# Retention in a six-block decoder: 16-bit parts for queries, keys and state, centring on ScalarE, row factors on GpSimd

## The chip, the cores and the metric

The kernel runs on one core of one Trainium2 chip. The metric is the device time of the whole program in microseconds (us). Three runs of the kernel before gave 1024.1, 1029.05 and 1029.89 us, median 1029.05 us.

## The reference

The program is a two-layer decoder over x of 2 sequences x 1024 tokens x 256 features. Each layer adds an attention, a cross attention and a feed-forward block to x, each on the layer-normalised x. The change touches only the attention of the second layer, a retention:

```
q, k (scaled), v, g = x @ q_w + q_b, ...      # 16 heads; q, k 16 wide, v 32 wide
qr, kr = theta_shift(q), theta_shift(k)       # x*cos + rotate_every_two(x)*sin
qk = einsum(qr, kr) * mask                    # mask: causal decay per head, rows scaled by 1/sqrt(row sum)
denom = clip(|sum of the row of qk|, 1, None)
out = einsum(qk / denom, v)
out = (out - mean) / sqrt(var + 1e-5)         # over each head's 32 values
return (silu(g) * out) @ o_w + o_b
```

## The kernel before

The function `retention` (line 2608) works through 16 tiles of 128 tokens, eight per sequence. Within a tile it makes the causal scores of all 16 heads; what lies further back comes through a running state `us` of key-value products, kept per head and decayed once a tile (recurrent form across tiles, attention form inside one). The decay mask is folded into the cosine and sine tables, so only an upper-triangle clearing is left for GpSimd.

All engines are programmed by hand, each with its own loop `for s in STEPS` from -2 to 18, and meet through semaphores (`wait_ge` and `then_inc`). **Each engine runs its own list in order**: an instruction that waits holds up everything behind it in that list. A step `s` works on several tiles at once (a software pipeline): the projections of tile s+2, the turned queries and keys of s+1, the scores of s, the outputs of s-1, the gate of s-2, the output projection of s-3.

- TensorE (lines 3026 to 3043): `score(s,0)`, `weigh(s-1)`, `qk(s+2)`, `score(s,1)`, `turn_qk(s+1,0)`, `output(s-3)`, `turn_qk(s+1,1)`, `values(s+1)`, `delta(s)`, `turn_z(s-2)`, `turn_x(s+4)`, `gates(s-1)`. `score` (L2922) multiplies 32-bit `qkT` by head; half 0 and half 1 of the heads share one PSUM tile `pss`, so half 1 waits for `lo_done`, the end of VectorE's `low(s,0)`. `weigh` (L2941) applies the scores, and L2937 applies the state copy `u` in 32 bits. `delta` (L3022) makes the new key-value products. `turn_qk` (L2996) transposes 32-bit `rot`.
- ScalarE (lines 2885 to 2902): `high(s,0)` (L2852, the high 16-bit part of the scores), `squares(s-1)` (L2843, L2845), `high(s,1)`, two `copy_turned` (L2859), `values(s+1)` (L2867 a 16-bit and L2868 a 32-bit copy), `z_high`, `x_high`, `silu(s-1)` (L2879).
- VectorE (lines 2812 to 2833): `low(s,0)` (L2726, the low part of the scores), `x_center(s+5)` (L2492), `gate(s-2)` (L2749, L2752), `rotate(s+2)` (L2779 to L2785), `low(s,1)`, `centre(s-1)` (four operations, L2762 to L2767, that make variance plus floor), `state(s)` (L2795, L2798), `add`, `z_low`, `values_low(s+1)` (L2734), `x_low`.
- GpSimd (lines 2707 to 2713): `mask(s,0)` and `mask(s,1)` (L2686, two instructions each), `power(s-1)` (L2705: (variance + floor) to the power -1/2, 16 numbers a partition), `expand(s)` (L2695: the state spread into the block layout `u`).

`high(s,j)` waits for the scores, `low(s,j)` for `high(s,j)`, `mask(s,j)` for `low(s,j)`, `weigh(s)` for both masks, and the second product of `gate` for `power`. DMA plays a part only at the start of the stage, for the tables.

Of the kernel before, what the change touches and what calls it, by code (L numbers as in the profile page):

```python
# [11 lines left out]
F16 = mybir.dt.float16  # L12
# [2358 lines left out]
def tables():  # L2371
# [16 lines left out]
    floor = lay(EPS * total)  # L2388
# [5 lines left out]
class Ahead:  # L2394
# [6 lines left out]
    def __init__(self, nc, ctx, signals, x):  # L2401
# [15 lines left out]
        self.normed, self.turned = sem("normed"), sem("turned")  # L2417
# [76 lines left out]

    def turn(self, t_, t, ps):
# [36 lines left out]
    def on_vector(self, v, own, event, added, ps):  # L2532
# [50 lines left out]
    def on_scalar(self, a, event, ps):  # L2583
# [7 lines left out]
        if event == (1, 5):  # L2591
# [3 lines left out]
            a.mul(self.bhi[r, 0:D], self.brow[r], GAIN).then_inc(self.b_high, 1)  # L2595
            a.mul(self.b16[0:1, 0:D], self.brow[0:1], GAIN).then_inc(self.b_high, 1)
# [11 lines left out]
def retention(nc, x, ins, ahead, opening):  # L2608
# [3 lines left out]
    with ExitStack() as ctx:  # L2612
# [12 lines left out]
        rfloor, keep = sb("rfloor", [P, TB, HR]), sb("keep", [P, 4])  # L2625
        rowtile = sb("rowtile", [P, 4])
        rb = sb("rb", [P, 512])
        rot = sb("rot", [P, ROTS, 2, HR, 2 * KD])
        qkT = sb("qkT", [P, 2, 2, 4, P])
        v32 = sb("v32", [P, 2, HR, VC])  # L2630
        v16 = sb("v16", [P, 2, 2, HR, VC], F16)
        att = sb("att", [P, 2, 2, 4, 4, P], F16)
        u, us = sb("u", [P, 2, 4, 4, VC]), sb("us", [P, 2, 4, VC])
# [7 lines left out]
        names = ("qk_ready rot_done q_turned q_copied k_turned k_copied v_psum v_done "  # L2641
                 "g_psum silu_done scored hi_done lo_done kept_state masked vhi_done vlo_done d_ready u_done pv_done cen_done sq_done sq_used centred pow_done "
                 "z_ready z_turned zhi_done z_split o_ready x_added").split()
        (qk_ready, rot_done, q_turned, q_copied, k_turned, k_copied, v_psum, v_done,
         g_psum, silu_done, scored, hi_done, lo_done, kept_state, masked, vhi_done, vlo_done, d_ready, u_done, pv_done, cen_done, sq_done, sq_used, centred, pow_done,
# [15 lines left out]
        def _(sp):  # L2661
            for dst, nm in ((rfloor, "floor"), (keep, "keep")):
                sp.dma_start(dst[:], ins["ret_" + nm]).then_inc(s_norm, 16)
# [5 lines left out]
        def _(g):  # L2669
            own = Tally(g, s_g)  # L2670
            g.memset(rot[:, :, :, :, KD:2 * KD], 0.0).then_inc(s_c, 1)
            g.memset(v32[:, :, :, VD:VC], 1.0).then_inc(s_c, 1)
            g.memset(v16[:, :, 0, :, VD:VC], 1.0).then_inc(s_c, 1)
            g.memset(v16[:, :, 1, :, VD:VC], 0.0).then_inc(s_c, 1)
            own.link(g.memset(rowtile[:], 0.0))
            for h in range(4):
                own.link(g.memset(rowtile[32 * h:32 * h + 32, h:h + 1], 1.0))
            ahead.power(g, 2)
# [11 lines left out]
            def expand(t):  # L2690

                if inside(t) and t % TB != TB - 1:
                    g.wait_ge(kept_state, t + 1)
                    wait(g, pv_done, t)
                    g.tensor_tensor(u[:, (t + 1) % 2], us[:, t % 2].unsqueeze(2).broadcast_to((P, 4, 4, VC)),  # L2695
                                    rowtile[:].unsqueeze(1).unsqueeze(3).broadcast_to((P, 4, 4, VC)), ALU.mult).then_inc(u_done, 1)
                elif inside(t):
                    g.wait_ge(kept_state, t + 1)
                    g.tensor_copy(tiny[:], us[:, t % 2, 0, 0:1]).then_inc(u_done, 1)

            def power(t):
                if inside(t):
                    q = t % 2
                    g.wait_ge(centred, t + 1)
                    g.tensor_tensor(sm[:, q, 2, :], sm[:, q, 1, :], ahead.sm[:, 4, 0:1].broadcast_to((P, HR)), ALU.pow).then_inc(pow_done, 1)  # L2705

            for s in STEPS:
# [3 lines left out]
                expand(s)  # L2711
# [4 lines left out]
        def _(v):  # L2716
# [12 lines left out]
            def values_low(t):  # L2729
                if inside(t):  # L2730
                    q = t % 2
                    v.wait_ge(vhi_done, t + 1)
                    v.wait_ge(v_done, t + 1)
# [945 lines left out]
```

## Time and profile before

| | us |
|---|---|
| median of three runs | 1029.05 |
| profiled execution, its own time | 1025.94 |
| its span | 1024.1 |
| retention, first instruction to last | 505.83 to 719.77 |

| engine | busy us, share of the span | busy us in 533.05 to 702.81 |
|---|---|---|
| TensorE | 874.4 (85%) | 167.72 of 169.76 |
| VectorE | 784.2 (77%) | 145.26 |
| ScalarE | 615.7 (60%) | 90.71 |
| GpSimd | 372.5 (36%) | 117.15 |

Times in timelines are us from the start of the span. The first column is the start, the second the time from the start of the row's first instruction to the end of its last. The engines are PE (TensorE; PEld its weight loads), DVE (VectorE), ACT (ScalarE) and POOL (GpSimd). A bracket gives the idle time before the row and who ended it.

### The profile page before, as it was taken

To read this page: it belongs to the slowest core of one execution; us is meant where nothing else is said; L and a number is where in the kernel's file an instruction comes from. 1 tells how busy PE (TensorE), PEld (TensorE's weight loads), DVE (VectorE), ACT (ScalarE), POOL (GpSimd) and SP (SyncE) were. 2 spreads that over 40 slices of the span, in tenths; PEclk is the share of its full clock that TensorE was granted. 3 is DMA by queue.
4 is the path that set the end of the run, shared out by engine and by line. 5 is a ranking of instruction groups with operands and counts; after the bars stand their busy time and mean duration, and the time that the engine had idled before them with its cause. 6 is when DMAs were issued, how large, how long until landed. Compare 5 with 4: busy or idle time off the path is not lost. (4 is left out here: it accounts for less than half of the span.)

```text
span 1024.1 us, 22180 instructions
## 1 busy us (share of the span) xinstructions
PE 874.4 (85%) x8762; PEld 579.5 (57%) x8762; DVE 784.2 (77%) x1460; ACT 615.7 (60%) x1108; POOL 372.5 (36%) x326
## 2 busy tenths in 40 slices
PE   1386878788488899999689999998799998999997
PEld 0122323232246555565356777776689975778786
DVE  8899989833788899887678899887577886667443
ACT  5578789887476554452155555554578865656431
POOL 1043435321247140000246667666144641224220
PEclk9998889898679899999899999999799999999999
DMA  5403232320420030000120000000200000000000
GB/s 148 83 1 48 36 54 32 48 37 1 135 72 1 2 135 1 1 2 1 58 111 1 3 2 2 2 3 2 73 2 2 2 1 1 2 12 11 12 22 31
DMA packets 21670, 30.47 MB, mean 30 GB/s; under 512 B 6000, under 2 KB 17982, under 8 KB 20416
## 3 DMA queue, kind: packets, MB, share of 16 engines
q1 hardware_dynamic: 18816, 26.44, 11.2%
q10 hardware_dynamic: 2752, 2.62, 0.9%
q8 instruction: 70, 1.15, 0.5%
q14 instruction: 32, 0.26, 0.1%
HBM read 18.56 MB, written 2.10 MB: 20 GB/s over the span
## 5 line engine op out<-in xcount | busy, mean ns | idle before, releaser
L589 ACT ACTIVATE t_pT<-t_sc 128x1536 f32<-128x1536 f32 x96 | 136.7, 1454 | 28.8 <-PE t_sc L696 28.5
L269 POOL TENSOR_SCALAR_AFFINE_SELECT t_pT<-t_pT 128x512 f32<-128x512 f32 x64 | 75.9, 1206 | 167.4 <-ACT t_pT L589 167.3
L696 PE MATMUL t_sc<-t_qk 32*128 32x512 f16 (+3 forms) x1152 | 89.1, 365 | 47.4 <-DMA t_qk<-t_sin_parts 26.6
L696 PEld LDWEIGHTS t_sc<-t_qk 32*128 32x128 f16 x1152 | 37.1, 99 | 107.0 <-issue 50.4
L2686 POOL TENSOR_SCALAR_AFFINE_SELECT r_att<-r_att 128x1024 f16<-128x1024 f16 x64 | 69.5, 1108 | 66.2 <-DVE r_att L2726 66.2
L717 PE MATMUL t_ot<-t_pT,t_v 128*17 128x512 f32 (+3 forms) x768 | 81.3, 535 | 11.3 <-DVE t_ou L433 5.1
L1983 PE MATMUL c_pso<-ck_VO,c_pT 128*128 128x256 f16 x480 | 55.0, 273 | 1.4 <-DVE c_pT L1824 1.4
L2726 DVE TENSOR_TENSOR r_att<-r_pss,r_att 128x1024 f16<-128x1024 f32 x32 | 39.1, 1221 | 20.2 <-ACT r_att L2852 20.2
L1983 PEld LDWEIGHTS c_pso<-ck_VO,c_pT 128*128 128x128 f16 x480 | 46.3, 98 | 6.7 <-DVE c_pT L1824 1.6
L2268 ACT ACTIVATE m_sg<-m_psg 128x512 f32<-128x512 f32 x32 | 19.1, 596 | 51.6 <-PE m_psg L2311 51.5
L2852 ACT CAST r_att<-r_pss 128x1024 f16<-128x1024 f32 x32 | 32.4, 1012 | 28.0 <-PE r_pss L2922 28.0
L1894 ACT ACTIVATE c_pt<-c_pss,c_mx 128x154 f32<-128x154 f32 x128 | 48.4, 415 | 1.1 <-DVE c_mx L1807 1.1
L2332 PE MATMUL m_acc<-gw_down,m_hp 128*128 128x256 f16 x384 | 47.2, 273 | 1.9 <-DVE m_hp L2224 1.4
L2948 PE MATMUL r_psv<-ra_w,ra_xT 128*128 128x512 f16 x192 | 46.8, 380 | 1.0 <-ACT r_v L2868 1.0
L2705 POOL TENSOR_TENSOR r_sm<-r_sm,ra_sm 128x16 f32<-128x16 f32 x16 | 46.3, 2895 | 3.6 <-DVE r_sm L2767 2.0
L717 PEld LDWEIGHTS t_ot<-t_pT,t_v 128*17 128x17 f32 x768 | 17.5, 102 | 51.8 <-issue 37.6
L1774 POOL TENSOR_TENSOR c_pn<-c_pt,c_tot 128x208 f32<-128x208 f32 x16 | 24.1, 1507 | 58.3 <-DVE c_tot L1814 58.3
L2332 PEld LDWEIGHTS m_acc<-gw_down,m_hp 128*128 128x128 f16 x384 | 36.9, 98 | 12.4 <-DVE m_hp L2224 2.0
L2922 PEld LDWEIGHTS r_pss<-r_qkT 32*128 32x128 f32 x512 | 31.0, 186 | 13.6 <-issue 11.2
L2922 PE MATMUL r_pss<-r_qkT 32*128 32x128 f32 x512 | 37.1, 283 | 1.0 <-DVE r_att L2726 1.0
L2859 ACT COPY r_qkT<-r_ptr 128x512 f32<-128x512 f32 x32 | 18.8, 588 | 29.7 <-PE r_ptr L2996 29.7
L1824 DVE TENSOR_TENSOR c_pT<-c_pst,c_pT 128x512 f16<-128x512 f32 (+1 forms) x48 | 28.7, 598 | 10.3 <-ACT c_pT L1905 9.4
(593 smaller groups left out, 2408.7 us busy)
## 6 DMA issues: line engine op xcount, KB each, us to landing
t_qk<-t_cos_parts SPq DMA_DIRECT2D x24, 128.0 KB, 5.4
t_qk<-t_sin_parts SPq DMA_DIRECT2D x24, 128.0 KB, 7.0
x<-in_x ACTq DMA_DIRECT2D x4, 512.0 KB, 7.3
out_x<-x SPq DMA_DIRECT2D x8, 256.0 KB, 2.1
r_rcos<-in_ret_cos SPq DMA_DIRECT2D x1, 1280.0 KB, 9.1
r_rsin<-in_ret_sin SPq DMA_DIRECT2D x1, 1280.0 KB, 10.6
t_qk<-t_cos_parts SPq DMA_DIRECT2D x16, 64.0 KB, 2.7
gw_raw<-in_gateT SPq DMA_DIRECT2D x1, 1024.0 KB, 7.6
```

The source lines that it names most:

```text
L269: last = g.affine_select(out=blk, in_=blk, compare_op=ALU.is_ge, fill=0.0, base=0, pattern=[[0, 4], [1, P]], channel_multiplier=-1)
L589: a.activation(pT[:, at:at + 3, :].rearrange("p a s -> p (a s)"), sc[s % 2][:], ACT.Exp, scale=CURVE * CURVE / math.sqrt(2 * DH)).then_inc ...
L696: last = t.matmul(sc[s % 2][:, 512 * k + at:512 * k + at + w], qk[r, g % 3, 1, of_k, P * i:P * i + P], qk[r, g % 3, 0, of_q, q0:q0 + w], s ...
L717: last = t.matmul(ot[j][32 * h:32 * h + DH + 1, 512 - w:512], v1[:, b, 4 * c + h, i, :], pT[:, (4 * slot + h) % RING, at:at + w], start=be ...
L1894: last = a.activation(pt[:, q, h, :], pss[:, k, n * CTX:n * CTX + CTX], ACT.Exp, bias=mx[:, q, 3 * k + n:3 * k + n + 1], scale=1.0, accum_ ...
L1983: last = mm(pso[:, 0:D], l, r, start=(n == 0), stop=(n == len(todo) - 1))
L2332: last = mm(acc[:, j, :], hp[:, k, ph_, P * j:P * j + P], dw[:, pw, D * e:D * e + D], start=(e == 0 and j % 2 == 0 and ph_ + pw == 0), sto ...
L2686: last = g.affine_select(out=blk, in_=blk, compare_op=ALU.is_ge, fill=0.0, base=0, pattern=[[0, 8], [1, P]], channel_multiplier=-1)
L2705: g.tensor_tensor(sm[:, q, 2, :], sm[:, q, 1, :], ahead.sm[:, 4, 0:1].broadcast_to((P, HR)), ALU.pow).then_inc(pow_done, 1)
L2726: v.tensor_tensor(att[:, t % 2, 1, 2 * j:2 * j + 2].rearrange("p h g m -> p (h g m)"), pss[:].rearrange("p j m -> p (j m)"), att[:, t % 2, ...
L2922: last = mm(pss[:, j, P * g:P * g + P], qkT[r, q, 1, g, :], qkT[r, q, 0, g, :], start=(g == 0), stop=True, skip_group_check=True)
L2948: last = mm(d, l, r, start=(i == 0), stop=(i == len(todo) - 1))
```

## The change

Queries and keys after rotation, and the state, are held as two 16-bit parts (high and low) in place of one 32-bit number, and products are formed from pairs of parts. `x_center` moves from VectorE to ScalarE, the factors' small operations from VectorE to GpSimd, and the spreading of the state from GpSimd to ScalarE. The factor 1/32 of the variance is folded into constants.

```diff
@@ GpSimd
-            def expand(t):
+            def split_state(t):
                 if inside(t) and t % TB != TB - 1:
                     g.wait_ge(kept_state, t + 1)
-                    wait(g, pv_done, t)
-                    g.tensor_tensor(u[:, (t + 1) % 2], us[:, t % 2].unsqueeze(2).broadcast_to((P, 4, 4, VC)), rowtile..., ALU.mult).then_inc(u_done, 1)
+                    wait(g, u_done, t)
+                    own.link(g.tensor_copy(us16[:, t % 2, 0], us[:, t % 2]))
+                    g.tensor_tensor(us16[:, t % 2, 1], us[:, t % 2], us16[:, t % 2, 0], ALU.subtract).then_inc(us_split, 1)
+            def swap(t):
+                if inside(t):
+                    keys, swap_ = rot[:, t % ROTS, 1], rot[:, t % ROTS, 2]
+                    g.wait_ge(rot_low, t + 1)
+                    g.tensor_copy(swap_[:, :, 0:KD], keys[:, :, KD:2 * KD])
+                    g.tensor_copy(swap_[:, :, KD:2 * KD], keys[:, :, 0:KD]).then_inc(swapped, 1)
             def power(t):
-                    g.wait_ge(centred, t + 1)
-                    g.tensor_tensor(sm[:, q, 2, :], sm[:, q, 1, :], ..., ALU.pow).then_inc(pow_done, 1)
+                    g.wait_ge(cen_done, t + 1)
+                    own.link(g.tensor_tensor(low_, cen[:, q, :, VD], rfloor[:, t % TB, 0, :], ALU.mult))
+                    own.link(g.tensor_tensor(low_, low_, low_, ALU.mult))
+                    own.link(g.tensor_scalar(low_, low_, 1.0, None, ALU.max))
+                    own.link(g.tensor_tensor(low_, low_, rfloor[:, t % TB, 1, :], ALU.mult))
+                    g.wait_ge(sq_used, t + 1)
+                    own.link(g.tensor_tensor(var, var, low_, ALU.add))
+                    g.tensor_tensor(sm[:, q, 2, :], var, ..., ALU.pow).then_inc(pow_done, 1)
             for s in STEPS:
                 mask(s, 0)
                 mask(s, 1)
                 power(s - 1)
-                expand(s)
+                swap(s + 2)
+                split_state(s)
@@ VectorE
-                x_center(s + 5)
                 gate(s - 2)
                 rotate(s + 2)          # its last sum now stays in psq
                 low(s, 1)
+                rotated_low(s + 2)     # psq - high part -> rot, 128x512 f16
                 centre(s - 1)          # now only the tensor_reduce
+                values_low(s + 1)      # now reads psv; before it stood after z_low
                 state(s)
@@ ScalarE
+            def expand(t):
+                if inside(t):
+                    a.wait_ge(us_split, t + 1)
+                    wait(a, pv_done, t)
+                    for h in range(4):
+                        last = a.activation(u[:, (t + 1) % 2, :, :, h, :], us16[:, t % 2], ACT.Copy, scale=rowtile[:, h:h + 1])
+                    last.then_inc(u_done, 1)
             for s in STEPS:
                 high(s, 0)
                 squares(s - 1)
                 high(s, 1)
+                rotated_high(s + 2)    # psq -> rot, waits for rot_done
                 copy_turned(s + 1, 0, q_turned, q_copied)
                 copy_turned(s + 1, 1, k_turned, k_copied)   # now 128x1024 f16
                 values(s + 1)          # the 32-bit copy is gone
                 z_high(s - 2)
                 x_high(s + 4)
                 silu(s - 1)
+                x_center(s + 5)
+                expand(s)
@@ TensorE
+  score: 16 instead of 8 products a half, f16 (keys, then keys with their parts swapped, against queries)
+  weigh: the state in two f16 products instead of one f32
+  turn_qk: 4 + 8 f16 transposes instead of 4 + 4 f32; the second group also waits for swapped
+  delta: 64 f16 products instead of 16 f32; waits for swapped
+  qk, turn_x, values, gates wait for rot_low or vlo_done instead of rot_done or v_done
```

## Rows read from the trace of the kernel before

**Rows 1.** The page: busy us, share of the span and instructions of each engine.

```profile
PE 874.4 (85%) x8762; PEld 579.5 (57%) x8762; DVE 784.2 (77%) x1460; ACT 615.7 (60%) x1108; POOL 372.5 (36%) x326
```

**Rows 2.** Busy time by window: PE, PEld, DVE, ACT, POOL, granted clock, DMA.

```profile
533.05:702.81 169.76, 167.72 (x2296) 121.51 (x2294) 145.26 (x270) 90.71 (x149) 117.15 (x86) 1.00 0.01 2
```

**Rows 3.** Timeline of one step, TensorE, ScalarE and VectorE (start, us, idle before).

```profile
586.29 1.16 PE L2922 MATMUL r_pss<-r_qkT 32*128 32x128 f32 x16
...
587.38 0.49 PE L2937 MATMUL r_pso<-r_u,r_qkT 128*128 128x132 f32 x2
...
587.55 1.01 ACT L2852 CAST r_att<-r_pss 128x1024 f16<-128x1024 f32 x1 [0.57 <-PE r_pss L2922]
...
588.60 1.22 DVE L2726 TENSOR_TENSOR r_att<-r_pss,r_att 128x1024 f16<-128x1024 f32 x1 [1.29 <-ACT r_att L2852]
...
589.74 0.40 DVE L2492 TENSOR_SCALAR ra_xn<-x,ra_sm 128x255 f32<-128x255 f32 x1
...
590.06 0.69 DVE L2749 TENSOR_TENSOR r_psv<-r_psv,r_cen 128x512 f32<-128x512 f32 x1
...
591.39 0.41 DVE L2779 TENSOR_TENSOR r_rb<-r_psq,r_rsin 128x256 f32<-128x256 f32 x1
...
592.34 0.66 PE L2996 MATMUL r_ptr<-ra_ident,r_rot 128*128 128x128 f32 x4
...
592.83 1.47 PE L2982 MATMUL r_psd<-ra_wo,r_zT 128*128 128x256 f16 x12
...
593.51 1.21 DVE L2726 TENSOR_TENSOR r_att<-r_pss,r_att 128x1024 f16<-128x1024 f32 x1
...
594.14 0.27 PE L2982 MATMUL r_psd<-ra_b,ra_one 128*128 128x256 f16 x1
```

**Rows 4.** Timeline of GpSimd: the second masks of tiles 0, 1, 15, and one step.

```profile
523.95 2.13 POOL L2686 TENSOR_SCALAR_AFFINE_SELECT r_att<-r_att 128x1024 f16<-128x1024 f16 x2 [1.33 <-DVE r_att L2726]
...
533.05 2.13 POOL L2686 TENSOR_SCALAR_AFFINE_SELECT r_att<-r_att 128x1024 f16<-128x1024 f16 x2 [1.50 <-DVE r_att L2726]
...
594.80 2.14 POOL L2686 TENSOR_SCALAR_AFFINE_SELECT r_att<-r_att 128x1024 f16<-128x1024 f16 x2 [2.66 <-DVE r_att L2726]
597.04 2.89 POOL L2705 TENSOR_TENSOR r_sm<-r_sm,ra_sm 128x16 f32<-128x16 f32 x1
599.90 1.07 POOL L2695 TENSOR_TENSOR r_u<-r_us,r_rowtile 128x528 f32<-128x528 f32 x1
...
702.81 2.13 POOL L2686 TENSOR_SCALAR_AFFINE_SELECT r_att<-r_att 128x1024 f16<-128x1024 f16 x2 [1.46 <-DVE r_att L2726]
```

**Rows 5.** Timeline, GpSimd's small operations at the start of the stage.

```profile
507.67 0.54 POOL L2677 MEMSET r_rowtile<- 32x1 f32 x4
508.43 1.01 POOL L2468 TENSOR_TENSOR ra_sm<-ra_sm 128x4 f32<-128x4 f32 x1 [0.23 <-DVE ra_sm L2483]
```

**Rows 6.** Line 1055, GpSimd's copies (ns min/median/max, first and last start).

```profile
L1055 POOL COPY ra_wo<-ra_b x4: 225/226/1288, 313.9 to 322.9; 64x52 f16<-64x52 f16 x4
```

**Rows 7.** Groups in 506 to 715: busy us, mean ns, idle before (ScalarE).

```profile
L2506 ACT CAST ra_xT<-r_psq 128x256 f16<-128x256 f32 x12 | 4.6, 382 | 0.0
...
L925 ACT ACTIVATE ce_room<-x,ce_room 128x256 f32<-128x256 f32 x4 | 2.3, 601 | 0.0
```

**Rows 8.** Timeline, first steps: the clock's slow stretch and the first scores.

```profile
511.08 2.72 PE L2948 MATMUL r_psq<-ra_w,ra_xT 128*128 128x512 f16 x6 [3.18 <-DVE r_rot L2785]
...
515.44 1.46 PE L2948 MATMUL r_psv<-ra_w,ra_xT 128*128 128x512 f16 x6
...
518.04 1.01 ACT L2852 CAST r_att<-r_pss 128x1024 f16<-128x1024 f32 x1
```

**Rows 9.** Timeline, the last tile.

```profile
707.67 0.60 ACT L2843 COPY r_cen<-r_pso 128x528 f32<-128x528 f32 x1 [1.83 <-PE r_pso L2941]
...
713.55 0.69 DVE L2752 TENSOR_TENSOR r_z<-r_psv,r_sm 128x512 f32<-128x512 f32 x1
...
719.35 0.42 DVE L2803 SCALAR_TENSOR_TENSOR x<-r_psd,x 128x256 f32<-128x256 f32 x1 [3.05 <-PE r_psd L2982]
```

More of the change, by code:

```diff
@@ L2738, in x_low @@
                     ahead.low(v, t, psq)
-            def x_center(t):
-                if inside(t) and t >= FIRST:
-                    ahead.center(v, t)
             def gate(t):
@@ L2821, in _ @@
                 z_low(s - 2)
-                values_low(s + 1)
                 x_low(s + 4)
@@ L2883, in x_high, with x_center @@
                     ahead.high(a, t, psq)
+            def x_center(t):
+                if inside(t) and t >= FIRST:
+                    ahead.center_on_scalar(a, t)
             for s in STEPS:
@@ L2921, in score @@
                             r = slice(32 * h, 32 * h + 32)
-                            last = mm(pss[:, j, P * g:P * g + P], qkT[r, q, 1, g, :], qkT[r, q, 0, g, :], start=(g == 0), stop=True, skip_group_check=True)
+                            mm(pss[:, j, P * g:P * g + P], qkT[r, q, 1, g, :], qkT[r, q, 0, g, :], start=(g == 0), stop=False, skip_group_check=True)
+                        for j in range(2):
+                            h = 2 * half + j
+                            r = slice(32 * h, 32 * h + 32)
+                            last = mm(pss[:, j, P * g:P * g + P], qkT[r, q, 2, g, :], qkT[r, q, 0, g, :], start=False, stop=True, skip_group_check=True)
                     last.then_inc(scored, 1)
@@ L2936, in weigh @@
                         if t % TB:
-                            mm(pso[:, bank, c0:c0 + 4 * VC], qkT[:, q, 0, g, :], u[:, q, g].rearrange("p h d -> p (h d)"),
-                               start=(g % 2 == 0), stop=False, skip_group_check=True)
+                            for part in range(2):
+                                mm(pso[:, bank, c0:c0 + 4 * VC], qkT[:, q, 0, g, :], u[:, q, part, g].rearrange("p h d -> p (h d)"),
+                                   start=(g % 2 == 0 and part == 0), stop=False, skip_group_check=True)
                         for h in range(4):
@@ L2994, in turn_qk @@
                         t_.wait_ge(q_copied, t + 1)
-                    for g in range(4):
-                        last = t_.transpose(ptr[:, P * g:P * g + P], rot[:, t % ROTS, n, 4 * g:4 * g + 4, :].rearrange("p h d -> p (h d)"), ahead.ident[:])
+                        t_.wait_ge(swapped, t + 1)
+                    for which in (0,) if n == 0 else (1, 2):
+                        for g in range(4):
+                            to = P * (4 * (which // 2) + g)
+                            last = t_.transpose(ptr16[:, to:to + P], rot[:, t % ROTS, which, 4 * g:4 * g + 4, :].rearrange("p h d -> p (h d)"), id16[:])
                     last.then_inc(done, 1)
@@ L3016, in delta @@
                     q = t % 2
-                    t_.wait_ge(v_done, t + 1)
-                    t_.wait_ge(rot_done, t + 1)
+                    t_.wait_ge(vlo_done, t + 1)
+                    t_.wait_ge(swapped, t + 1)
                     wait(t_, kept_state, t)
                     for g in range(4):
-                        for h in range(4):
-                            last = mm(psd[32 * h:32 * h + 32, VC * g:VC * g + VC], rot[:, t % ROTS, 1, 4 * g + h, :], v32[:, q, 4 * g + h, :],
-                                      start=(g == 0), stop=True, skip_group_check=True)
+                        for which, part in itertools.product((1, 2), range(2)):
+                            for h in range(4):
+                                last = mm(psd[32 * h:32 * h + 32, VC * g:VC * g + VC], rot[:, t % ROTS, which, 4 * g + h, :], v16[:, q, part, 4 * g + h, :],
+                                          start=(g == 0 and which == 1 and part == 0), stop=(which == 2 and part == 1), skip_group_check=True)
                     last.then_inc(d_ready, 1)
```

122 lines of the change are left out of this document (71 added, 51 removed).

## The prediction

> **What bounds the kernel now.** First the page's busy shares: TensorE 85%, VectorE 77% [rows 1]. Then the window of the steady retention steps: TensorE is busy for 167.72 of 169.76 us, VectorE for 145, GpSimd for 117, ScalarE for 91, at full clock [rows 2]. So TensorE is the bound there and the others have room, GpSimd least to spare after VectorE. Last, the timelines, for the order: the second mask of tile 1 starts at 533.05 and that of tile 15 at 702.81 [rows 4], so fourteen steps take 12.13 us each on average. GpSimd's second mask follows VectorE's second `low` at once (593.51 to 594.80, with 2.66 us of idle before it) [rows 3, 4]. The retention is some 214 of 1024 us; nothing else in the program changes but a few constants.
>
> **TensorE's work falls.** A half of `score` takes 1.09 us (586.29 to 587.38); twelve 256-column f16 products take 1.31 us, 0.109 each, so 0.055 for 128 columns (estimate) [rows 3]. Sixteen f16 products of which pairs run side by side make 8 x 0.055 = 0.44 us: -0.65 a half, -1.3 a step. The four state products in f16 twice over I put at -0.5, the transposes at -0.2, `delta` with 64 products in place of 16 at +0.4 (it could be +1.6 if each took the 0.1 of a 256-column one for itself; it could be 0). Together -1.6 us a step (-2.0 to -0.4). VectorE loses `x_center` (0.3) and three small operations and gains `rotated_low` (about 0.7, as other 128x512 differences): near -1. If TensorE stayed the bound this would be worth having. I don't think it does.
>
> **A loop closes through ScalarE's list.** Before, GpSimd alone spread the state, at the end of its step (599.90 [rows 4]), and only `weigh` two steps on needs it: it had most of a step in hand. Now `expand(s)` is the last thing in ScalarE's step s, it waits for `us_split`, and `us_split` comes from the last thing in GpSimd's step s, behind both masks, `power(s-1)` and `swap(s+2)`. Queued behind it on ScalarE is `high(s+1,0)`, and for that wait VectorE's `low(s+1,0)`, then everything behind it in VectorE's list (`gate(s-1)`, `rotate(s+3)`) and `low(s+1,1)`, which releases GpSimd's `mask(s+1,1)`. Nothing in this ring can be reordered, so a step can't be shorter than its sum:
>
> - `high(.,0)` start to `low(.,0)` start, 587.55 to 588.60: 1.05 [rows 3]
> - `low(.,0)` start to `low(.,1)` start, 588.60 to 593.51: 4.91, less `x_center`, 589.74 to 590.06, which leaves: 4.59 [rows 3]. The second half's scores (0.44) and `high(.,1)` (1.05) run beside `gate` and `rotate` and are ready earlier.
> - `low(.,1)` start to the second mask's start, 593.51 to 594.80: 1.29 [rows 3, 4]
> - masks, 594.80 to 597.04: 2.24; the power, 597.04 to 599.90: 2.86 [rows 4]
>
> That is 12.03 us from rows alone, already the old period, before any new instruction of the ring is counted. New in it:
>
> - Five small linked operations of `power` on 16 numbers. The trace has no such product. Below: four tiny fills in 0.54 us, 0.15 apart [rows 5], 0.75 in all. Above: the power of 4 numbers takes 1.01, of 16 numbers 2.89 [rows 4, 5], 0.157 a number, which leaves 0.38 for an instruction without numbers; with the hand-over 0.5, 2.6 in all. I take 0.38 each, nearest to that remainder: 1.9.
> - `swap`, two copies of 256 f16. Below 0.28 each (the 52-number copy, 0.226, and a gap [rows 6]); above 0.72 (0.2, and 256 at the 2.03 ns a number that the 528-number product takes in all, 1.07 [rows 4]). That product less 0.38 gives 1.3 ns a number: 0.2 + 0.25 = 0.45 each, 0.9.
> - `split_state`, a copy and a linked difference of 132: 0.35 + 0.5 = 0.85 (0.56, two of the short copies, to 1.3, two at 0.2 + 132 x 2.03 ns and two hand-overs). The state itself (`kept_state`) is there some 4 us after `low(s,1)` starts, the power later, so it isn't waited for.
> - `expand`, four ScalarE operations of 264 numbers with a factor per partition: between the plain 256-number copy, 0.382 less 0.1 of overlap, and the 256-number one with factor and offset, 0.601 [rows 7]: 1.1 to 2.4. I take 0.4 each: 1.6, and 0.1 for the hand-over.
>
> Together 5.35 (3.0 to 7.8, ends rounded), so the period is 12.03 + 5.35 = 17.4 us (15.0 to 19.8) against 12.13.
>
> For the four operations the Trainium skill has a price of its own (ScalarE: Activation LUTs, "What ACT_TABLE_LOAD costs"): 186 ns plus 0.833 ns an element, some 93 ns more for a per-partition operand, and neighbours overlap by about 93 ns. That gives 0.41 us each, and the sum would stay as it is; the 0.601 of rows 7, with two such operands, agrees with it within 0.03. Against the move of elementwise work to GpSimd speaks the GPSIMD Engine Reference of the Trainium skill, "Engine selection": VectorE for two-input work, GpSimd about twice as slow, one-input work near line rate. By its rates (about 2.6 cycles an element for two inputs, one for one input, at 1.2 GHz), without the cost of dispatch, swap and split would take some 0.8 us in place of 1.75, and the sum would be 16.4 a step; the trace's 2.0 ns an element for the 528-number product (1.07 us) lies near the page's 2.2.
>
> **The sum.** Fourteen steps (tile 1 to tile 15) x (17.4 - 12.13) = +73.8 us. From tile 0 to tile 1 it was 523.95 to 533.05, 9.1 us [rows 4]; there is no power and no gate yet, so the ring is 17.4 - 1.9 - 2.86 - 1.4 = 11.2: +2.1. Before tile 0: `rotated_high(1)` stands ahead of the copy of tile 0's queries and waits for the rotation of tile 1, and that rotation starts later since `qk(1)` waits for `rot_low`; I put the first `high` (518.04 [rows 8]) at 520.7: +2.6 (0 to 4). Last tile: `squares(15)` stood 4.86 us after the second mask's start (707.67 [rows 9], 702.81 [rows 4]). It now stands behind `expand(15)`: 2.24 + 1.9 + 2.86 + 0.2 + 1.7 = 8.9 us after it; reduction, sum and power (5.1 us from there) put the second gate product at 14.0 in place of 713.55 - 702.81 = 10.74: +3.3. All in all +81.8 us. On the profiled execution's own 1025.94 us (3.1 below the median) that is 1107.7; I say 1107.
>
> **Where the saved time goes.** TensorE will stand idle in front of `score(s,1)`, which waits for `low(s,0)`: about 17.4 - 10.5 = 7 us less what the copies of turned queries hold it up. VectorE waits for the first `high`. So the -1.6 buys nothing.
>
> **Rivals.**
> - *The ring holds and TensorE's clock falls as well.* After idle TensorE ran six products in 2.72 us (511.08) that take 1.46 at full clock (515.44) [rows 8], half speed, 1.2 in place of 2.4 GHz. With idle time in every step this can return each time. It matters if the whole chain from `score(s,1)` by the transposes, `values`, `delta`, `gates`, `silu(s-1)` to `expand(s)` runs slow: my walk gives 18.5 us a step, +1.1 x 14 = +15: 1123. For it: the idle per step is longer than the 3.18 us there. Against: at full clock `silu` is through 2 us before `us_split`, so a slow first part is hidden. The Trainium skill (TensorE: Matmul & The Clock Gate, "What's actually happening") says an idle array is halved by a gate until it has been busy again; by that alone the slow part comes back each step, and it costs the price just given only if it lasts to `gates`.
> - *TensorE stays the bound: faster.* One mechanism: `us_split(s)` comes before ScalarE gets to `expand(s)`, since the small GpSimd instructions are nearly free and the power of 16 numbers runs beside its followers. Then the step is 12.13 - 1.6 + 0.5 (the keys' turn waits behind `rotated_high`) = 11.0: 15 x -1.1 + 3 = -14, 1012. It decides if the ring is below 11 us; against it stands that the rows alone give 12.03.
> - *No change:* GpSimd's parts prove so short that ring and TensorE's saving cancel, a step of about 12.1 and 1029.
>
> **How the numbers follow.** The forecast (ring, full clock) 0.72; ring with slow clock 0.13; faster 0.10; no change 0.05. Predicted 1107. The forecast's own bounds: 15.0 a step gives 14 x 2.9 + 6 = +47, 1073; 19.8 gives 14 x 7.7 + 12 = +119, 1145. The range is 1068 to 1145; it leaves out the two last cases, 0.15. About 0.5%, 5 us, is what can be told from no change. Slower by more 0.85, within 0.05, faster 0.10.
>
> **What would show it.** In the profile after: ScalarE's first `high` (128x1024) of each step right behind the four `expand` instructions, and those with idle before them that GpSimd's difference ended, 1 us or more; second masks 17.4 us apart; the power directly followed by two copies and the split; TensorE idle before the second score half, ended by VectorE's `low`; TensorE busy no more than 11 of 17.4 us. Wrong would be: masks 11 to 12 us apart, `expand` without idle before it, or its wait ended by `weigh`. If the period is right but the small operations aren't 0.38, the size of that term falls, not the ring.

## The result: 6.8% slower, and where the time went

| | before | after |
|---|---|---|
| median, us (fastest to slowest run) | 1028.01 (1024.1 to 1029.89) | 1097.74 (1095.94 to 1098.95) |
| profiled span, us | 1024.1 | 1096.5 |
| tile 0's second mask | 523.95 | 529.16 |
| tile 1's second mask | 533.05 | 542.49 |
| tile 15's second mask | 702.81 | 771.21 |
| next stage's first GpSimd instruction | 721.24 | 792.52 |
| TensorE's mean granted clock over the span | 0.949 | 0.913 |

The ratio is 1.068, 95% interval 1.065 to 1.072. The times of the four marks split the 72.4 us by which the span grew: +5.2 up to tile 0, +4.2 from tile 0 to 1, +59.0 over the fourteen steady steps (228.72 in place of 169.76 us), +2.9 in the tail, +1.1 in all that follows. One run of e11 below, 1439.28 us at a mean granted clock of 0.564 where its others have 0.94 or more, is left out of its ratio.

The page's line of busy times of the kernel after, to be held against [rows 1]:

```profile
PE 881.3 (80%) x9338; PEld 565.6 (52%) x9338; DVE 767.9 (70%) x1418; ACT 655.5 (60%) x1184; POOL 394.2 (36%) x452
```

No engine's share has risen, so the shares don't name what made the program slower. The window of the fourteen steps (columns as in [rows 2]: PE, PEld, DVE, ACT, POOL, granted clock, DMA):

```profile
542.49:771.21 228.72, 170.52 (x2766) 108.42 (x2767) 129.50 (x232) 124.64 (x213) 136.50 (x196) 0.85 0.01 2
```

TensorE was busy for 167.72 of 169.76 us [rows 2]; now it is for 170.52 of 228.72, and that at a granted clock of 0.85. Every engine stands idle for a quarter of the time or more. So the step is set by a chain over several engines. This is one step of the kernel after, in order of time (the step that ends with tile 6's second mask, as in [rows 3, 4]):

```profile
608.85 2.13 POOL L2701 TENSOR_SCALAR_AFFINE_SELECT r_att<-r_att 128x1024 f16<-128x1024 f16 x2 [2.44 <-DVE r_att L2758]
610.96 0.22 POOL L2730 TENSOR_TENSOR r_sm<-r_cen,r_rfloor 128x16 f32<-128x16 f32 x1
...
612.49 2.92 POOL L2736 TENSOR_TENSOR r_sm<-r_sm,ra_sm 128x16 f32<-128x16 f32 x1
...
615.37 0.39 POOL L2721 COPY r_rot<-r_rot 128x256 f16<-128x256 f16 x1
...
616.05 0.29 POOL L2710 CAST r_us<-r_us 128x132 f16<-128x132 f32 x1
...
616.42 0.44 POOL L2711 TENSOR_TENSOR r_us<-r_us 128x132 f16<-128x132 f32 x1
...
616.90 1.73 ACT L2907 ACTIVATE r_u<-r_us,r_rowtile 128x264 f16<-128x264 f16 x4 [0.91 <-POOL r_us L2711]
...
618.53 0.99 ACT L2882 CAST r_att<-r_pss 128x1024 f16<-128x1024 f32 x1
...
619.55 1.23 DVE L2758 TENSOR_TENSOR r_att<-r_pss,r_att 128x1024 f16<-128x1024 f32 x1 [4.19 <-ACT r_att L2882]
...
620.84 0.23 PE L2977 MATMUL r_pss<-r_qkT 32*128 32x128 f16 x2 [2.34 <-DVE r_att L2758]
...
624.15 1.21 DVE L2758 TENSOR_TENSOR r_att<-r_pss,r_att 128x1024 f16<-128x1024 f32 x1
...
625.43 2.13 POOL L2701 TENSOR_SCALAR_AFFINE_SELECT r_att<-r_att 128x1024 f16<-128x1024 f16 x2 [2.43 <-DVE r_att L2758]
```

Read it as a loop. From 610.96 on GpSimd goes through its list without idle time (of the five small operations the first is shown, of the two copies too); ScalarE's `expand` (L2907) waited 0.91 us for GpSimd's last one; `high` follows at once, `low` waited 4.19 us for `high`, TensorE's second score half 2.34 us for `low`; the second `low` releases the second mask. From mask to mask there is no gap, and it took 16.58 us.

### The profile page after: what moved, and what is told of

It reads as the page before. It is cut to its first block and busy times, and to the rows that moved or that the text cites. A ratio compares the mean times of both kernels' runs of the same rounds, so it can differ in the third digit from the quotient of the medians.

```text
span 1096.5 us, 23523 instructions
## 1 busy us (share of the span) xinstructions
PE 881.3 (80%) x9338; PEld 565.6 (52%) x9338; DVE 767.9 (70%) x1418; ACT 655.5 (60%) x1184; POOL 394.2 (36%) x452
## 5 line engine op out<-in xcount | busy, mean ns | idle before, releaser
L717 PE MATMUL t_ot<-t_pT,t_v 128*17 128x512 f32 (+3 forms) x768 | 81.8, 537 | 11.1 <-DVE t_ou L433 5.0
L3008 PE MATMUL r_psv<-ra_w,ra_xT 128*128 128x512 f16 x192 | 60.6, 464 | 0.7 <-DVE r_v L2765 0.6
L2977 PE MATMUL r_pss<-r_qkT 32*128 32x128 f16 x256 | 19.8, 230 | 37.8 <-DVE r_att L2758 37.8
L3059 PE MATMUL r_ptr<-r_id,r_rot 128*128 128x128 f16 x192 | 20.4, 257 | 29.6 <-ACT r_qkT L2890 29.6
L2765 DVE SCALAR_TENSOR_TENSOR r_v<-r_psv,r_v 128x512 f16<-128x512 f32 x16 | 11.1, 694 | 42.1 <-ACT r_v L2916 42.1
L2977 PEld LDWEIGHTS r_pss<-r_qkT 32*128 32x128 f16 x256 | 12.4, 99 | 51.9 <-DVE r_att L2758 44.8
```

The source lines that it names most:

```text
L717: last = t.matmul(ot[j][32 * h:32 * h + DH + 1, 512 - w:512], v1[:, b, 4 * c + h, i, :], pT[:, (4 * slot + h) % RING, at:at + w], start=be ...
L3008: last = mm(d, l, r, start=(i == 0), stop=(i == len(todo) - 1))
```

## The experiments

All are set against the kernel before on the same chip. A step is the time from one second mask to the next. TensorE's six 512-column products of a projection serve as a reading of the clock: 1.46 us at full clock (2.4 GHz), up to 2.77 where part or all of them ran at 1.2 GHz.

**e1: `expand` a step later, at the same place.**

```diff
@@ ScalarE
                 x_center(s + 5)
-                expand(s)
+                expand(s - 1)
```

> ScalarE spreads the state one step later, expand(s-1) in place of expand(s), at the same place in its list; nothing is left out. Theory (two rings): the ring over GpSimd (16.58 us a step in the profile after) is cut, but ScalarE's own list stays a ring: from low(s,1) by rotated_high, the copy of the queries, the keys' turn, values, delta, gates, silu(s-1) and x_center to expand (8.4 us after low(s,1) starts), then 1.63 for expand, 1.02 and 4.60 to the next low(s,1): 15.7 us a step, 0.9 less than now. 14 x 0.9 = 13: about 1085. Rival 1 (the wait on GpSimd alone was the price, and TensorE becomes the bound at 11 us a step): about 1020. Rival 2 (the time is in the 16-bit work itself): 1097, no change.

Measured: 1077.02 us (1075.29 to 1077.68), ratio 1.048 (1.044 to 1.052). After a first step of 17.44 us and up to the last two (12.69 and 12.95) the steps lie between 14.39 and 15.77 us. So the ring through GpSimd's list was real: with the wait for the split of the same step gone, 0.8 to 2.2 us a step come back, 20.7 us in all where 13 were expected. The theory's 15.7 us was worked out from rows at the low clock; the windows of single steps show a granted clock of 0.89 in those of 15.1 to 15.8 us and of 1.00 in those of 14.4. But the step doesn't fall to 12.13: another loop stands right behind, and e2 shows it more cleanly.

**e2: the state's split ahead of the power.**

```diff
@@ GpSimd
                 mask(s, 1)
+                split_state(s)
                 power(s - 1)
                 swap(s + 2)
-                split_state(s)
```

> GpSimd's list reordered: split_state(s) right behind the masks, then power(s-1) and swap(s+2); nothing is left out. This takes 5.1 us (1.53 of small operations, 2.88 of the power, 0.68 of swap) out of the ring over GpSimd. Theory (two rings): the second ring, over ScalarE's own list, takes over at 15.7 us a step, so only 0.9 of the 5.1 comes back: about 1085. Rival 1 (one ring, every us out of it counts): 16.58 - 5.1 + about 2 of waiting for the state = 13.5 a step, about 1055. Rival 2 (16-bit work): 1097.

Measured: 1069.81 us (1067.17 to 1070.64), ratio 1.041 (1.036 to 1.045). That is 15 us less than expected, in the main for the reason given with e1. After two first ones of 16.07 and 16.29 us two steps of 14.4 us are followed by one of 15.56, three times over (the third of the long ones is 15.07), and the last three are shorter. ScalarE, TensorE and the split in a step of the long kind:

```profile
600.30 0.58 ACT L2897 CAST r_rot<-r_psq 128x512 f16<-128x512 f32 x1 [1.84 <-DVE r_psq L2804]
...
601.43 0.62 PE L3059 MATMUL r_ptr<-r_id,r_rot 128*128 128x128 f16 x8 [2.28 <-ACT r_qkT L2890]
601.89 2.39 PE L3008 MATMUL r_psv<-ra_w,ra_xT 128*128 128x512 f16 x6
...
606.61 0.44 POOL L2711 TENSOR_TENSOR r_us<-r_us 128x132 f16<-128x132 f32 x1
...
607.43 0.58 ACT L2927 ACTIVATE r_psv<-r_psv 128x512 f32<-128x512 f32 x1 [0.65 <-PE r_psv L3008]
...
608.42 1.72 ACT L2907 ACTIVATE r_u<-r_us,r_rowtile 128x264 f16<-128x264 f16 x4
```

The split is done 1.4 us before ScalarE gets to `expand` (607.05 against 608.42), so that wait is gone. What is left is a second ring: `rotated_high` waits for VectorE's rotation (1.84), the queries' copy stands behind it in ScalarE's list, TensorE waits 2.28 us for that copy, and then come the keys' turn, values, delta, gates, `silu`, `x_center`, `expand`, `high`, `low`, rotation. In this ring the clock counts: after the 2.28 us of idle, values took 2.39 in this step and 1.46 in those of 14.40 us.

**e3: as e1, and `expand(s - 1)` into the gap behind `high(s,1)`.**

```diff
@@ ScalarE
                 high(s, 1)
+                expand(s - 1)
                 rotated_high(s + 2)
...
                 x_center(s + 5)
-                expand(s)
```

> expand(s-1), placed between high(s,1) and rotated_high(s+2) in ScalarE's list, where the profile after shows ScalarE idle for 1.84 us; nothing is left out. Theory: the four instructions (1.73 us) hide there and both rings lose them; what is left is low(s,1) to silu and x_center (8.4 us, less if TensorE's clock stays up) + 1.02 + 4.60 = 14.0 us a step at the clock of now, 12.7 at full clock: 1044 to 1062. Rival 1 (TensorE's bound of 11 us at once): 1015 to 1020. Rival 2 (16-bit work): 1097.

Measured: 1053.73 us (1051.88 to 1055.1), ratio 1.025 (1.020 to 1.030). After two first ones of 15.09 and 15.22 us, and up to the last two, the steps go to and fro with the clock: where values took 1.46 us the step is 12.42 to 12.85, where they took 2.2 to 2.8 us it is 13.95 to 14.45, close to the 12.7 and 14.0 expected for the two clocks. The 1.63 us of `expand` is out of both rings and fills ScalarE's wait for the rotation.

**e4: the five small operations back on VectorE, only the power on GpSimd.**

```diff
@@ GpSimd, power(t)
-                    g.wait_ge(cen_done, t + 1)
-                    own.link(g.tensor_tensor(low_, cen[:, q, :, VD], rfloor[:, t % TB, 0, :], ALU.mult))
...
-                    own.link(g.tensor_tensor(var, var, low_, ALU.add))
+                    g.wait_ge(centred, t + 1)
@@ VectorE, centre(t)
+                    L(v.tensor_tensor(low_, cen[:, q, :, VD], rfloor[:, t % TB, 0, :], ALU.mult))
...
+                    v.tensor_tensor(var, var, low_, ALU.add).then_inc(centred, 1)
```

> One part of the change undone: the five small operations of the row factors are made by VectorE, within centre(s-1), as in the kernel before; GpSimd keeps the power alone. Nothing is left out. It takes 1.53 us out of the ring over GpSimd. Theory (two rings): the ring over ScalarE's list caps the gain at 0.9 us a step: about 1085. Rival 1 (one ring): 14 x 1.53 = 21 less, about 1076. Rival 2 (these operations hidden beside other work): 1097.

Measured: 1092.86 us (1091.14 to 1096.11), ratio 1.064 (1.059 to 1.069); steps of 16.50 us, where 1.53 us out of a ring of 16.58 leave 15.05. A miss. GpSimd and VectorE of that step:

```profile
620.50 2.13 POOL L2701 TENSOR_SCALAR_AFFINE_SELECT r_att<-r_att 128x1024 f16<-128x1024 f16 x2 [2.43 <-DVE r_att L2751]
620.95 0.67 DVE L2784 TENSOR_TENSOR r_sm<-r_cen,r_rfloor 128x16 f32<-128x16 f32 x1
621.65 1.01 DVE L2785 TENSOR_TENSOR r_sm<-r_sm 128x16 f32<-128x16 f32 x1
...
622.90 0.17 DVE L2787 TENSOR_TENSOR r_sm<-r_sm,r_rfloor 128x16 f32<-128x16 f32 x1
623.11 0.69 DVE L2789 TENSOR_REDUCE r_sm<-r_sq 128x16 f32<-128x512 f32 x1
623.83 0.17 DVE L2791 TENSOR_TENSOR r_sm<-r_sm 128x16 f32<-128x16 f32 x1
...
624.09 2.90 POOL L2729 TENSOR_TENSOR r_sm<-r_sm,ra_sm 128x16 f32<-128x16 f32 x1 [1.46 <-DVE r_sm L2791]
```

VectorE's products of 16 numbers take 0.17 us (L2787), but 0.67 and 1.01 while GpSimd's masks run: the first ends at 621.62, when the first of the two mask instructions is through (half of 2.13), the second at 622.66, when the second is (622.63). So VectorE's last sum came at 623.83 and the power, 3.59 us after the mask's start as against 3.64 in the kernel after, waited 1.46 us for it. Without the 1.34 us by which these two are longer than 0.17 the sum would have ended at about 622.7, just as the masks did (an estimate; no run shows it). The Trainium skill (SBUF — State Buffer, "SBUF: two separate sides") says that a VectorE operation with two SBUF inputs and a GpSimd operation that reads SBUF exclude each other for a whole instruction. For the masks the trace agrees. For the power it doesn't: in the kernel after, VectorE's second product of `state` (L2824, both inputs in SBUF) takes 0.29 or 0.30 us beside the power, in each of the thirteen steps where they meet, and 0.75 where it meets a mask:

```profile
613.31 0.29 DVE L2824 TENSOR_TENSOR r_us<-r_us,r_keep 128x132 f32<-128x132 f32 x1
...
772.74 0.75 DVE L2824 TENSOR_TENSOR r_us<-r_us,r_keep 128x132 f32<-128x132 f32 x1
```

**e5: as e3, and the queries' copy first.**

```diff
@@ ScalarE
                 high(s, 1)
-                expand(s - 1)
-                rotated_high(s + 2)
                 copy_turned(s + 1, 0, q_turned, q_copied)
+                expand(s - 1)
+                rotated_high(s + 2)
```

> Against the e3 kernel (1053.7), ScalarE copies the turned queries first and then does the four expand operations and rotated_high. Theory (second ring): in e3 TensorE stood 2.3 us in front of the keys' turn because the queries' copy stood behind rotated_high and so behind VectorE's rotation; with the copy ahead of both, the keys' turn, values, delta, gates and silu come about 1.4 us earlier (now held by the keys' copy behind rotated_high): steps of 12.5 us in place of 13.9, 1034 (1027 to 1042). Rival (VectorE's list or GpSimd's holds the step in e3): the idle time of TensorE only moves, 1052 to 1055.

Measured: 1017.4 us (1015.29 to 1018.56), ratio 0.991 (0.988 to 0.994): 0.9% below the kernel before, little but clear of the noise. The steps are 11.48 us; I had expected 12.5 and 1034, so the direction was right and the gain almost twice as large. With the idle time in front of the keys' turn gone, TensorE's clock stayed up as well: of e3 (first) and e5 (second), the same window, columns as above.

```profile
560.00:680.00 120.00, 101.64 (x1719) 65.26 (x1717) 84.44 (x153) 80.93 (x141) 82.53 (x119) 0.91 0.01 2
```

```profile
560.00:680.00 120.00, 109.83 (x2100) 74.10 (x2099) 102.11 (x187) 91.42 (x162) 102.31 (x150) 1.00 0.01 3
```

In e5 TensorE is busy 109.83 of 120 us, 10.5 us a step of 11.48, at full clock.

**e6: as e5, `x_center` ahead of `silu`.**

```diff
@@ ScalarE
-                silu(s - 1)
                 x_center(s + 5)
+                silu(s - 1)
```

> As e5_queries_first, and x_center stands ahead of silu, where ScalarE was idle 0.84 us waiting for the gates' projection, in place of between silu and the next high. Theory (the ring over ScalarE's list): high starts 0.5 us earlier a step, 7 us less than e5, 1027 (1018 to 1035). Rival: the gap is gone once the queries' copy comes early, so silu is late by what high gains: within 2 us of e5.

Measured: 1017.57 us (1016.19 to 1020.27), ratio 0.992 (0.989 to 0.994), steps of 11.48: no difference from e5, a miss. `high(s+1,0)` did start earlier, 2.11 us behind the gates' start in place of 2.49, but its `low` already ended before TensorE was through with `qk`, so nothing followed from it. The ring of e5 and e6 goes another way. Rows of e5, TensorE, ScalarE and VectorE:

```profile
637.08 0.57 ACT L2897 CAST r_rot<-r_psq 128x512 f16<-128x512 f32 x1
...
638.45 0.62 ACT L2916 ACTIVATE r_v<-r_psv 128x512 f16<-128x512 f32 x1
...
639.10 0.69 DVE L2765 SCALAR_TENSOR_TENSOR r_v<-r_psv,r_v 128x512 f16<-128x512 f32 x1
...
639.85 1.47 PE L3008 MATMUL r_psv<-ra_w,ra_xT 128*128 128x512 f16 x6 [0.34 <-DVE r_v L2765]
...
645.53 1.01 ACT L2882 CAST r_att<-r_pss 128x1024 f16<-128x1024 f32 x1 [0.76 <-PE r_pss L2981]
...
646.92 1.74 ACT L2907 ACTIVATE r_u<-r_us,r_rowtile 128x264 f16<-128x264 f16 x4
```

`rotated_high`, the keys' copy, the values' copy, its low part, gates; behind them on TensorE, without a gap, `score(s+1,0)`, `weigh`, `qk` and `score(s+1,1)`; then `high`, the queries' copy (646.44), `expand`, and the next `rotated_high` at 648.56, 11.48 us after the first. `x_center` isn't in it, `expand` is.

**e7: GpSimd's swap made twice in the kernel after.**

```diff
@@ GpSimd, swap(t)
+                    for again in range(2):
                         g.tensor_copy(swap_[:, :, 0:KD], keys[:, :, KD:2 * KD])
+                        if not again:
+                            own.link(g.tensor_copy(swap_[:, :, KD:2 * KD], keys[:, :, 0:KD]))
```

> The kernel after, with GpSimd's two swap copies made twice (0.68 us of copies more in each step up to that of tile 13, the output unchanged). Theory (the ring through GpSimd's list has no slack): each of some 14 steps grows by 0.7 to 0.75 us, 1108 (1105 to 1111), idle before expand grows by as much. Rival (the period is set by ScalarE's and TensorE's chain, GpSimd only nearly as long): 1098 to 1101.

Measured: 1107.73 us (1107.47 to 1108.95), ratio 1.079 (1.077 to 1.082), 10.0 us above the kernel after. GpSimd's copies and what follows:

```profile
598.58 0.40 POOL L2722 COPY r_rot<-r_rot 128x256 f16<-128x256 f16 x1
...
599.38 0.40 POOL L2722 COPY r_rot<-r_rot 128x256 f16<-128x256 f16 x1
...
600.07 0.30 POOL L2710 CAST r_us<-r_us 128x132 f16<-128x132 f32 x1
...
600.92 1.73 ACT L2910 ACTIVATE r_u<-r_us,r_rowtile 128x264 f16<-128x264 f16 x4 [2.97 <-POOL r_us L2711]
```

From the first copy to the split it is 1.49 us in place of 0.68 (615.37 to 616.05), so 0.81 more, and the steps are 17.41 in place of 16.59: 0.82 more. Each added microsecond on GpSimd was a microsecond of the step. That is the ring without slack, shown by a dose.

**e8: e2, with TensorE kept busy in front of the keys' turn.**

```diff
@@ TensorE
                 output(s - 3)
+                filler(s + 1)      # from tile 4: 16 products of 256 columns into psv, overwritten by values
                 turn_qk(s + 1, 1, k_turned)
```

> The e2 kernel (split before power, 1069.8) with 16 products of 256 columns more in TensorE's idle time of 2.3 us in front of the keys' turn, from tile 4 on; their result is overwritten by values. Theory (half of the steps are longer because the clock is low in values after that idle time, 15.56 against 14.40 us): no values projection over 1.5 us, all steps 14.4, 4 us less, 1066 (1063 to 1068). Rival: the clock isn't what makes the steps differ, or the added products hold up the keys' turn: 1070 to 1080.

Measured: 1066.92 us (1065.82 to 1069.32), ratio 1.040 (1.037 to 1.042), 2.9 below e2. The runs of the two overlap, so the steps have to decide. From tile 4 on every values projection takes 1.46 us, and the long steps are gone: from tile 3 to tile 11 they are 14.40 us but for one of 14.47, then 13.91, 13.91 and 12.80. So the extra 1.16 us of e2's long steps was the clock. The last step took 15.95 us in place of e2's 12.84: there the added products ran at the low clock (2.93 us in place of 1.91) and held up the keys' turn.

**e9 and e10: `expand` before `silu`; then also the values' low part ahead of VectorE's reduction.**

```diff
@@ ScalarE (e9, against e5)
                 copy_turned(s + 1, 0, q_turned, q_copied)
-                expand(s - 1)
                 rotated_high(s + 2)
...
                 x_high(s + 4)
+                expand(s - 1)
                 silu(s - 1)
@@ VectorE (e10, against e9)
                 rotated_low(s + 2)
+                values_low(s + 1)
                 centre(s - 1)
-                values_low(s + 1)
```

> As e5_queries_first (1017.4, steps of 11.48), but the four expand operations stand between x_high and silu, where ScalarE was idle 1.17 us a step, in place of between the queries' copy and rotated_high. Theory: in e5 the step is the ring gates, score(s+1,0), weigh, qk, score(s+1,1), high, queries' copy, expand, rotated_high, keys' copy, values copy, low part of the values, gates; taking the 1.63 us of expand out of it lets the step shrink until VectorE's rotation or TensorE's 10.5 us of work holds it: 10.7 to 11.1 us, 1009 (1004 to 1014). Rival: expand delays silu and the weighing of the next tile by what it gives: 11.5 us, 1016 to 1019.

> As e9_expand_before_silu, and VectorE makes the low part of the values ahead of its 0.67 us reduction. Theory: gates waits for that part, so once expand is gone from ScalarE's side this reduction is in the ring: 0.2 to 0.5 us a step less, 1005 (1000 to 1010). Rival: the values copy on ScalarE is not there earlier, or the power is late: equal to e9 within 2 us.

Measured: e9 1019.47 us (1015.65 to 1020.73), ratio 0.990 (0.988 to 0.992); e10 1017.75 us (1017.55 to 1019.03), ratio 0.990 (0.989 to 0.991). Steps of 11.47 us in both: two misses, no difference from e5. ScalarE's list in e9:

```profile
639.15 0.59 ACT L2897 CAST r_rot<-r_psq 128x512 f16<-128x512 f32 x1 [1.29 <-DVE r_psq L2804]
...
642.16 1.74 ACT L2907 ACTIVATE r_u<-r_us,r_rowtile 128x264 f16<-128x264 f16 x4
...
643.80 0.59 ACT L2927 ACTIVATE r_psv<-r_psv 128x512 f32<-128x512 f32 x1
...
644.80 0.99 ACT L2882 CAST r_att<-r_pss 128x1024 f16<-128x1024 f32 x1
645.83 1.22 DVE L2758 TENSOR_TENSOR r_att<-r_pss,r_att 128x1024 f16<-128x1024 f32 x1 [1.71 <-ACT r_att L2882]
```

The 1.29 us of waiting for the rotation is back ahead of `rotated_high`, and `silu` now has no idle before it: `expand` had left one ring and joined another, by `silu`, `x_center`, `high(s+1,0)`, `low`, rotation and `rotated_high`. That two rings have the same length to 0.01 us was suspicious, hence the last of this line.

**e11: e10 with `expand` in two halves, one in each place.**

```diff
@@ ScalarE
                 copy_turned(s + 1, 0, q_turned, q_copied)
+                expand(s - 1, 0)       # h = 0, 1
                 rotated_high(s + 2)
...
-                expand(s - 1)
+                expand(s - 1, 2)       # h = 2, 3, then u_done
                 silu(s - 1)
```

> As e10_values_low_first (steps of 11.47), with two of the four expand operations between the queries' copy and rotated_high, where ScalarE is idle 1.3 us in e10, and two ahead of silu. Theory: two rings of nearly the same length go through ScalarE's list; the whole expand in the first makes e5's step (11.48), in the second e9's and e10's (11.47); halved, each loses 0.8 us, and TensorE's 10.5 us of work and its hand-overs hold the step: 10.8 us, 14 x 0.65 = 9 us less, 1009 (1006 to 1013). Rival: the three equal steps have one common cause that isn't expand's place (GpSimd, or TensorE's hand-overs): 11.4 to 11.5 us, 1016 to 1019.

Measured: 1013.56 us, ratio 0.987 (0.984 to 0.989), 13.5 us less than the kernel before; four runs lie between 1011.01 and 1015.78. Steps of 11.11 us (expected 10.8). Both theories of e9's and e10's equal steps were half right: `expand`'s place did hold them, but only 0.36 of the 0.65 us came. The trace shows what holds the step at 11.11 with TensorE busy 10.5 of it, though no run tests it:

```profile
626.46 1.47 PE L3010 MATMUL r_psv<-ra_w,ra_xT 128*128 128x512 f16 x6 [0.34 <-DVE r_v L2765]
...
634.78 0.59 ACT L2897 CAST r_rot<-r_psq 128x512 f16<-128x512 f32 x1 [0.32 <-DVE r_psq L2804]
```

It is one more ring, through three lists: `rotated_high` (623.67), the keys' and the values' copy, VectorE's low part of the values, the gates on TensorE, `silu`, `x_center`, `high(s+1,0)`, then VectorE's `low`, `gate` and rotation, and `rotated_high` again 11.11 us after the first; each waits for the one before it or stands right behind it.

**e12: the kernel after, with TensorE kept busy at both places where it was idle.**

```diff
@@ TensorE
                 qk(s + 2)
+                early(s)           # from tile 4: 16 products of 256 columns into psd, overwritten by output
                 score(s, 1)
...
                 output(s - 3)
+                filler(s + 1)      # as in e8
                 turn_qk(s + 1, 1, k_turned)
```

> The kernel after with 16 products of 256 columns more on TensorE ahead of the second score half and 16 more ahead of the keys' turn, from tile 4 on, where it was idle; their results are overwritten. Theory (the ring through GpSimd's list sets the step, TensorE's slow clock is hidden beside it): output and values run in 1.47 us each, the steps stay 16.6 us, 1097.7 (1096 to 1100). Rival (the slow clock carries part of the loss, since silu is only just through before the state's split): steps of 15.5 to 16.2 us, 1085 to 1093.

Measured: 1097.89 us (1095.76 to 1098.72), ratio 1.068 (1.066 to 1.071): no difference from the kernel after. The window in e12 and in the kernel after:

```profile
560.00:680.00 120.00, 104.89 (x1750) 74.67 (x1749) 70.65 (x130) 67.39 (x117) 72.36 (x103) 0.98 0.01 2
```

```profile
560.00:680.00 120.00, 90.67 (x1479) 56.91 (x1478) 69.20 (x126) 66.96 (x116) 72.18 (x106) 0.86 0.01 2
```

The clock went from 0.86 to 0.98 and the steps stayed at 16.6 (16.60 to 16.68, as before with one of 16.1 among them). From where the added products run, ScalarE's idle time before `expand` is 1.17 to 2.16 us in this window, against 0.40 to 2.07 in the kernel after. The kernel after shows the same by itself: its step from 658.10 has values in 1.46 us and the one above in 2.36, and both take 16.58. In the steady steps of the kernel after the slow clock costs nothing.

## Why the prediction was right, step by step

**The ring: right.** It was predicted by the order of four lists and found instruction by instruction; e7 shows that it has no slack, e1 and e2 that to open it gives time back. Its terms, from the starts shown above:

| part of the ring | predicted | measured | |
|---|---|---|---|
| first `high` to first `low` | 1.05 | 1.02 | 618.53, 619.55 |
| first to second `low` | 4.59 | 4.60 | 619.55, 624.15 |
| second `low` to second mask | 1.29 | 1.28 | 624.15, 625.43 |
| masks | 2.24 | 2.11 | 608.85, 610.96 |
| five small operations | 1.9 | 1.53 | 610.96, 612.49 |
| power | 2.86 | 2.88 | 612.49, 615.37 |
| `swap` | 0.9 | 0.68 | 615.37, 616.05 |
| `split_state` | 0.85 | 0.85 | 616.05, 616.90 |
| `expand` with hand-over | 1.7 | 1.63 | 616.90, 618.53 |
| sum | 17.4 | 16.58 | |

The terms read from rows of the trace before came out within 0.03 us but for the masks. The two most mis-sized terms are those that the trace before didn't show: a small operation costs 0.30 us with its link in place of 0.38 (the power's length cut back to no numbers was a poor stand-in; its cost a number isn't that of a product), and a copy of 256 numbers 0.34 in place of 0.45. Together they make 0.6 of the 0.8 us. Over fourteen steps 0.8 is 11.2 us; and the mean step was 16.34, since one in the middle took 16.09 and the last two (15.47 and 14.71) have less in them, another 3.4 us. That is +59.0 in place of +73.8.

**The ends: too low at the start.** The stage's marks in the kernel after, on GpSimd and VectorE:

```profile
529.16 2.13 POOL L2701 TENSOR_SCALAR_AFFINE_SELECT r_att<-r_att 128x1024 f16<-128x1024 f16 x2 [1.10 <-DVE r_att L2758]
...
534.36 0.30 POOL L2710 CAST r_us<-r_us 128x132 f16<-128x132 f32 x1 [2.38 <-DVE r_us L2824]
```

```profile
780.60 0.58 ACT L2873 COPY r_cen<-r_pso 128x528 f32<-128x528 f32 x1
...
785.91 0.69 DVE L2780 TENSOR_TENSOR r_z<-r_psv,r_sm 128x512 f32<-128x512 f32 x1 [1.17 <-issue]
...
792.52 0.52 POOL L1776 MEMSET c_pn<- 128x512 f32 x1 [6.70 <-POOLq L51]
```

Tile 0 to 1 took 13.33 us, +4.2 against the +2.1 predicted: the prediction took the power out of that ring but left the claim that the state is never waited for, and without the power to hide it the split waited 2.38 us for it. Most of this wait was the low clock, which is not free here: values just before it took 2.77 us. In e12, which has the same instructions up to this place, they took 1.46, and the wait is

```profile
532.55 0.30 POOL L2710 CAST r_us<-r_us 128x132 f16<-128x132 f32 x1 [0.69 <-DVE r_us L2824]
```

and tile 0 to 1 takes 11.65 us, +2.55. So 1.7 of the 2.1 us by which this was too low are the low clock, which costs time here because the state is waited for, and some 0.4 are left for that wait itself. Up to tile 0 it was +5.2 in place of +2.6 (1.2 of it the stage's later start, 507.06 in place of 505.83). In the tail, `squares(15)` came 9.39 us after the second mask (predicted 8.9) and the second gate product 14.70 (predicted 14.0), +4.0 in place of +3.3; of this 2.9 were left when the next stage began. So the ends cost 12.3 in place of 8.0, and 1.1 came after the stage: 5.4 of the 14.8 us by which the steps were overrated came back, and the span grew by 72.4 in place of 81.8 us. That the two errors have opposite signs is luck.

**TensorE's saving: right in size, lost as said.** Its work a step is 10.5 us at full clock (e5), and it was 167.72 / 14 = 12.0 in the kernel before: 1.5 less, where 1.6 was predicted. `score`'s sixteen products took 0.55 us (614.80 to 615.35 on TensorE) where eight in 32 bits, of which the trace records two each, took 1.09.

**The clock: right in cost, wrong in fact.** The forecast had full clock, with 0.72, against 0.13 for a slow one that costs 1.1 us a step. The clock did fall in every step: its granted mean lies between 0.75 and 0.90 in each of the fourteen, values took 2.36 us in the step above, and TensorE is busy for 12.5 of 16.58 us, not the "no more than 11" that the prediction named as a sign. What held was the reason given against the rival's price: ScalarE has slack before `expand`. It was thinner than the 2 us said, 0.05 to 2.07 over the fourteen steps and under 1 us in eight of them, as the first part ran slow; e12 shows that it was enough. That so thin a slack held in every step is in part luck. In e2, where the GpSimd ring is opened, the rival's price is paid, 1.16 us in a long step, and e8 takes it back.

**Signs.** `high` right behind `expand`, `expand`'s wait ended by the split, the power followed by two copies and the split, TensorE's wait for `low`: all there. "1 us or more" of idle before `expand` was there in six of the fourteen steps only.

**The faster rival** named the right place, the order in which ScalarE gets to `expand`, and a step of 11.0 with TensorE as the bound. The change as made doesn't reach it, but with another order of the same instructions it comes close: e5 and e11 run steps of 11.48 and 11.11, with TensorE busy 10.5 of them, and end 0.9% and 1.3% below the kernel before. The 6.8% were the price of where `expand` and the queries' copy stand, not of the 16-bit parts.

## What to carry to other kernels

Where engines run their lists in order, look for loops before you add up busy time: if the end of one engine's step waits for the end of another's, and the next step's first instruction is queued behind that wait, the step is the sum round the loop, however idle each engine is. Before giving up such a change, move the waiting instruction a step later and into a gap, and let nothing that another engine needs stand behind an instruction that itself waits (the queries' copy behind `rotated_high` made the difference between e3 and e5, 36 us). When one loop is opened the next is seldom far: here 16.58, then 14.40, 12.4 to 14.5, 11.48 and 11.11.

## What the runs showed of the hardware that I had not expected

- VectorE's operation on 16 numbers with two SBUF inputs took 0.67 and 1.01 us beside GpSimd's masks and 0.17 without (e4). Small work taken back from GpSimd was paid again as waiting. The trace of the kernel before shows it already: a product of `centre` takes 1.06 us in each of the fifteen steps with a mask beside it, and 0.17 for the last tile, where there is none:

```profile
702.87 1.06 DVE L2763 TENSOR_TENSOR r_sm<-r_sm,r_rfloor 128x16 f32<-128x16 f32 x1
...
708.86 0.17 DVE L2763 TENSOR_TENSOR r_sm<-r_sm,r_rfloor 128x16 f32<-128x16 f32 x1
```

- On GpSimd the same five operations took 0.21 to 0.25 us each, 0.30 to 0.33 from start to start with a semaphore between.
- TensorE's clock fell at different places under one order of work: in e2 two steps of 14.40 (values in 1.46 us) are followed by one of 15.56 (2.39 us), and in e3 from tile 6 on a long step and a short one take turns. The Trainium skill (TensorE: Matmul & The Clock Gate, "HAM oscillation — how this bites in real kernels") describes a loop in which TensorE is idle part of each round and so starts every round at the low clock. In e2 and e3 only every third and every second round pays; in e8, with the idle time filled, none does between tile 4 and tile 13.
